# One step a turn, one edge buffer: a graph layer's kernel on one core

## The reference, cut to what matters

```
agg = segment_sum(edge_attr_48, dst, 12500)          # 412500 edges x 48, dst is sorted
h   = relu(layernorm(x))                             # x: 12500 nodes x 128
in_ = concat([h, agg, graph_globals[0]], axis=1)     # 128 + 48 + 64 columns
out = x + relu(in_ @ W1 + b1) @ W2 + b2              # hidden 256, out 128, all fp32
```

## Time and profile before

| | us |
|---|---|
| median of 3 runs | 277.42 |
| the profiled execution | 277.42 |
| its span | 275.7 |
| busy: TensorE, VectorE, ScalarE, GpSimd | 243.9, 241.4, 146.3, 75.4 |

### The profile page before, as it was taken

One profiled execution on the slowest core, in us unless ns is written; L12 is line 12 of the kernel. 1 busy time (PEld: TensorE's weight loads), 2 busy tenths in 40 slices (PEclk: granted clock), 3 DMA queues, 4 the chain that ended last, 5 costly groups with the idle time before them and its releaser, 6 DMA issues.

```text
span 275.7 us, 17264 instructions
## 1 busy us (share of the span) xinstructions
PE 243.9 (88%) x7448; PEld 195.3 (71%) x7448; DVE 241.4 (88%) x579; ACT 146.3 (53%) x315; POOL 75.4 (27%) x89
## 2 busy tenths in 40 slices
PE   7344869989999999799999999999999998999893
PEld 5234757687787788588778778877887796787572
DVE  2977699979879998999999999999999999886394
ACT  3712156566577564556455555655565555456640
POOL 8473010402113203203302312311330330334210
PEclk9955599999999999999999999999999999999999
DMA  7999999999999999999999999999999999982101
GB/s 247 370 381 379 336 382 385 360 330 382 390 387 387 392 389 386 378 390 387 390 394 386 386 393 388 384 389 386 367 391 390 386 372 375 387 291 88 40 38 57
DMA packets 70876, 94.53 MB, mean 343 GB/s; under 512 B 4324, under 2 KB 64260, under 8 KB 70854
## 3 DMA queue, kind: packets, MB, share of 16 engines
q1 hardware_dynamic: 69802, 94.29, 95.6%
q10 hardware_dynamic: 956, 0.00, 0.2%
q0 software_dynamic: 96, 0.00, 0.0%
HBM read 87.88 MB, written 6.40 MB: 342 GB/s over the span
## 4 chain that ended last, share of the span: by engine, by line
DMA 60%; PE 16%; DVE 12%; issue 5%; SPq 2%; POOL 1%; ACT 0%; DVEq 0%; POOLq 0%
DMA out<-out_buf 56%; PE group_bank L1020 6%; DVE onehot L777 5%; DMA x_buf<-in_x 3%; PE out_bank L1086 3%; SPq L327 2%; PE hidden_bank L1068 2%; PE window_bank L1043 2%; DVE rel_rows L732 2%; POOL out_buf L514 1%; DMA dst_rows<-in_dst 1%; DVE tile_sums L840 1%; DVE bn L819 1%; PE hidden_bank L1004 1%; DVE placing L789 1%
## 5 line engine op out<-in xcount | busy, mean ns | idle before, releaser
L777 DVE TENSOR_TENSOR onehot<-rel,const_bank 128x896 f32<-128x896 f32 (+1 forms) x122 | 122.8, 1026 | 8.1 <-PE group_bank L1020 8.0
L1020 PE MATMUL group_bank<-edge_buf,onehot 128*32 128x48 f32 x6454 | 87.1, 211 | 9.9 <-DVE onehot L777 5.8
L1020 PEld LDWEIGHTS group_bank<-edge_buf,onehot 128*32 128x32 f32 x6454 | 79.9, 113 | 22.2 <-issue 12.3
L514 POOL TENSOR_TENSOR out_buf<-mlp_out,xb_buf 128x512 f32<-128x512 f32 x23 | 29.6, 1288 | 166.0 <-DMA out<-out_buf 137.1
L1068 PE MATMUL hidden_bank<-normed_t,w_node 128*128 128x512 f32 (+1 forms) x100 | 51.6, 597 | 0.8 <-issue 0.7
L1086 PE MATMUL out_bank<-w_sb,hidden 128*128 128x128 f32 x384 | 47.7, 277 | 1.4 <-ACT normed_t L587 1.4
L1086 PEld LDWEIGHTS out_bank<-w_sb,hidden 128*128 128x128 f32 x384 | 44.7, 192 | 1.6 <-issue 1.6
L576 ACT ACTIVATE normed_x<-x_buf,shift,inverse 128x128 f32<-128x128 f32 x98 | 40.3, 482 | 9.7 <-DVE shift L834 9.7
L1072 PE MATMUL hidden_bank<-tile_sums,w_high 112*128 112x512 f32 (+1 forms) x50 | 39.0, 781 | 0.0
L502 POOL TENSOR_TENSOR xb_buf<-x_buf,b_rows 128x512 f32<-128x512 f32 (+1 forms) x25 | 31.6, 1267 | 19.8 <-DMA x_buf<-in_x 10.3
L608 ACT ACTIVATE hidden<-hidden_bank,hidden_bias 128x512 f32<-128x512 f32 (+1 forms) x50 | 32.3, 670 | 4.3 <-PE hidden_bank L1074 4.2
(11 more groups left out here) (92 smaller groups left out, 218.1 us busy)
## 6 DMA issues: line engine op xcount, KB each, us to landing
edge_buf<-in_edge_attr SPq DMA_DIRECT2D x97, 672.0 KB, 10.4
edge_buf<-in_edge_attr SPq DMA_DIRECT2D x24, 504.0 KB, 10.3
x_buf<-in_x SPq DMA_DIRECT2D x24, 256.0 KB, 8.9
out<-out_buf SPq DMA_DIRECT2D x23, 256.0 KB, 9.4
dst_rows<-in_dst SPq DMA_DIRECT2D x3, 448.5 KB, 7.8
dst_rows<-in_dst SPq DMA_DIRECT2D x1, 252.3 KB
out<-out_buf SPq DMA_DIRECT2D x1, 224.0 KB
edge_buf<-in_edge_attr SPq DMA_DIRECT2D x1, 168.0 KB, 9.2
```

The lines of the kernel that those rows point to most:

```text
L514: pool.tensor_tensor(out_buf[k.parity][:, 0:nj, :], mlp_out[:, 0:nj, :], xb_buf[k.third][:, 0:nj, :], ALU.add).then_inc(out_added, 1)
L777: dve.tensor_tensor(onehot[:, c0:c0 + cols, :], rel[:, r0:r0 + cols].unsqueeze(2).to_broadcast([P, cols, WINDOW]), ramp_const.unsqueeze(1) ...
L1020: done = pe.matmul(group_bank[h][WINDOW * j:WINDOW * (j + 1), n * F_EDGE:(n + 1) * F_EDGE], onehot[:, (g0 + j) * EDGES_PER_ROW + r, :], ed ...
```

## The change: what it does

- There is one edge buffer. `load_quad(s, q)` waits for the use of quad q in step s-1.
- TensorE's loop has 24 turns of one step. Conditions on the turn's number pick what the first two turns do otherwise. The first layer of tile s-2 now comes before `turn_x` of tile s-1.
- `hidden`, `normed_t` and `tile_sums` are single, but for a copy of tile 23's; ScalarE waits for the layers of the tile before, and copies the turned x after `relu_hidden`.
- There are 16 output buffers, with a semaphore each; `add_out` waits for the store 16 tiles back.
- At step s SP issues part 0 of step s+1, the x tile s+1, the store of tile s-4, part 1 of step s+1. The index blocks 1 to 3, b2 and the weights are loaded among the quads of step 1 and the x tile of tile 1.
- The index blocks 1 to 3 are made relative, turned and copied in steps 0 and 1; TensorE turns them at the end of these.
- `tile_low` runs on GpSimd in steps 2 to 23, ahead of `add_out`; the last three stay on VectorE.
- VectorE loads the two window positions of a step ahead of its fifth one-hot, and its opening order changes.
- The opening matmuls on ones (`keep_clock`) become a loop.

```diff
...
-        self.value = c + 2 * i if self.static else i * 2 + c
+        self.value = i + c
...
-        edge_buf = [sb(f"edge_buf{p}", [P, GROUPS, ROW]) for p in range(2)]
+        edge_buf = sb("edge_buf", [P, GROUPS, ROW])
...
-        out_buf = [sb(f"out_buf{p}", [P, NJ, F_NODE]) for p in range(2)]
+        out_buf = [sb(f"out_buf{n}", [P, NJ, F_NODE]) for n in range(OUT_SLOTS)]
...
+        def own(k):
+            return 1 if k.static and k.value == tiles - 2 else 0
...
-                if not s.below(2):
-                    sp.wait_ge(edges_used, s.plus(-2).value * NQ + q + 1)
+                if not s.below(1):
+                    sp.wait_ge(edges_used, s.plus(-1).value * NQ + q + 1)
...
-            load_part(At(1), 0)
-            load_part(At(1), 1)
             sp.dma_start(b2_rows[:, :], bass.AP(tensor=b2.tensor, offset=0, ap=[[0, P], [1, F_NODE]]))\
               .then_inc(b2_in, 16)
+            load_dst(1)
+            load_part(At(1), 0)
+            load_weights()
+            load_part(At(1), 1)
+            load_dst(2)
             load_x(At(1))
-            for s in range(steps):
-                if s >= 1 and s + 1 < tiles:
+            load_dst(3)
+            for s in range(1, steps):
+                if s + 1 < steps:
+                    load_part(At(s + 1), 0)
+                if s < tiles - 1:
                     load_x(last_tile() if s + 1 == tiles - 1 else At(s + 1))
-                if s + 2 < steps:
-                    load_part(At(s + 2), 0)
-                if s == 0:
-                    load_weights()
-                if s >= 4:
+                if 4 <= s < full_steps:
                     store(At(s - 4))
-                if s + 2 < steps:
-                    load_part(At(s + 2), 1)
-                if 1 <= s + 1 < blocks:
-                    load_dst(s + 1)
+                if s + 1 < steps:
+                    load_part(At(s + 1), 1)
...
-                elif not k.below(2):
-                    pool.wait_ge(stored[k.parity], k.turn * 16)
+                elif not k.below(OUT_SLOTS):
+                    pool.wait_ge(stored[slot(k)], k.value // OUT_SLOTS * 16)
...
             for s in range(steps):
+                if 2 <= s < full_steps:
+                    pool.wait_ge(xb_ready, s)
+                    tile_low(At(s - 2))
+                    pool.wait_ge(tile_low_ready, s + 1)
                 if s >= 3:
                     add_out(At(s - 3))
...
             copy_sums(At(0), 1)
+            relative(1)
             deviate(At(0))
             normalise(At(0))
+            copy_rel(1)
             copy_sums(At(1), 0)
             copy_turned(At(0))
+            bias()
             deviate(At(1))
+            relative(2)
             copy_sums(At(1), 1)
             normalise(At(1))
+            copy_rel(2)
+            relative(3)
+            copy_rel(3)
             for s in range(2, full_steps):
...
-                copy_turned(At(s - 1))
-                if s == 2:
-                    bias()
                 deviate(At(s))
                 relu_hidden(At(s - 2))
+                copy_turned(At(s - 1))
                 copy_sums(At(s), 1)
...
-                if s >= 2:
-                    tile_low(At(s - 2))
                 moments(At(s))
...
                 make_onehot(n, 3)
+                base = [window_base(At(s), h) for h in range(2)]
                 make_onehot(n, 4)
...
-                for _ in range(n):
+                with pe.Fori(0, n):
                     pe.matmul(bank[:, 0:2 * P], ones16[:, 0:P], ones16[:, :], start=True, stop=True)
...
-            with pe.Fori(0, full_steps // 2) as i:
...
+            with pe.Fori(0, full_steps) as i:
+                step = At(0, i)
+                sum_part(step, 0)
+                with pe.If(i > 1):
+                    place(step.plus(-1), 1)
+                    pe.wait_ge(rel_ready, 2 * blocks)
+                    first_layer(step.plus(-2))
+                    turn_x(step.plus(-1))
+                with pe.Else():
+                    with pe.If(i > 0):
+                        place(At(0), 1)
+                        turn_x(At(0))
+                        sum_bias()
+                    with pe.Else():
+                        turn_places()
+                sum_part(step, 1)
+                place(step, 0)
+                with pe.If(i > 1):
+                    second_layer(step.plus(-2))
+                with pe.Else():
+                    pe.wait_ge(bias_ready, i * 2 + 1)
+                    turn_rel(i + 1)
+                    with pe.If(i > 0):
+                        turn_rel(3)
...
```

More of the change, by code:

```diff
@@ L19 @@
 LAST_GROUPS = 5
+OUT_SLOTS = 16
 TILE = 512
@@ L183, in gnn_kernel @@
         b2_in = sem("b2_in")
[L184 removed]
+        edges_in = [sem(f"edges_in{q}") for q in range(NQ)]
         x_in = [sem(f"x_in{p}") for p in range(2)]
[L186 removed]
+        stored = [sem(f"stored{n}") for n in range(OUT_SLOTS)]
         last_stored = sem("last_stored")
@@ L276, in agg_tile, with before_own, slot, stores_of @@
             return agg[:, :, bass.ds(tile_strip(k), P)]
+        def own(k):
+            return 1 if k.static and k.value == tiles - 2 else 0
+        def before_own(k):
+            return k.value - 1 if k.value_is_last and k.static else k.value
+        def slot(k):
+            return k.value % OUT_SLOTS if k.static else 0
+        def stores_of(n):
+            return len(range(n, tiles - 1, OUT_SLOTS)) + (n == (tiles - 2) % OUT_SLOTS)
         def sums_tile(k, row):
-            sums = tile_sums[k.parity][row:row + F_EDGE, 0:strips_of(k) * P]
+            sums = tile_sums[own(k)][row:row + F_EDGE, 0:strips_of(k) * P]
             if k.value_is_last:
@@ L399, in _ @@
             store_last(last_tile(), last_stored)
-            sp.wait_ge(stored[0], 16 * (tiles // 2))
-            sp.wait_ge(stored[1], 16 * (tiles // 2) + 16)
+            for n in range(OUT_SLOTS):
+                sp.wait_ge(stored[n], stores_of(n) * 16)
             sp.wait_ge(last_stored, 16)
@@ L550, in copy_rel @@
                                    .rearrange("p (r g) -> p r g", g=P)[:, :, 0:rows], ACT.Copy)\
-                        .then_inc(rel_ready, 2 * steps if (b, h) == (blocks - 1, 1) else 1)
+                        .then_inc(rel_ready, 1)
             def copy_sums(s, h):
@@ L595, in tile_high @@
                     act.wait_ge(agg_added, min(2 * k.value + 3, all_adds) + 3)
-                    if not k.below(2):
-                        act.wait_ge(hidden_ready, 2 * k.value - 2)
+                    if not own(k):
+                        act.wait_ge(hidden_ready, 2 * before_own(k))
                 act.activation(sums_tile(k, 0), agg_tile(k), ACT.Copy).then_inc(tile_high_ready, 1)
@@ L602, in relu_hidden @@
                     act.wait_ge(out_ready, k.value)
-                elif not k.below(2):
-                    act.wait_ge(out_ready, k.value - 1)
+                elif not own(k):
+                    act.wait_ge(out_ready, before_own(k))
                 for c in range(2):
@@ L915, in _ @@
             make_placing(At(steps - 1), 0)
+            last_base = window_base(At(steps - 1), 0)
+            dve.wait_ge(tile_low_ready, tiles - 3 + 2)
             tile_low(At(tiles - 3))
@@ L918, in _ @@
             invert(last)
-            add_window(At(full_steps - 1), 1)
+            add_window(At(full_steps - 1), 1, base[1])
             low_sums(At(steps - 1), 0)
-            add_window(At(steps - 1), 0)
+            add_window(At(steps - 1), 0, last_base)
             tile_low(second)
@@ L938, in _ @@
                 dve.sem_inc(general_added, 1)
-                dve.wait_ge(stored[0], 16 * (tiles // 2))
-                dve.wait_ge(stored[1], 16 * (tiles // 2) + 16)
+                for n in range(OUT_SLOTS):
+                    dve.wait_ge(stored[n], stores_of(n) * 16)
                 dve.wait_ge(last_stored, 16)
@@ L1035, in place @@
                 pe.wait_ge(placing_ready[h], s.value + 1)
-                if not s.below(1) or h == 1:
+                if not s.below(1):
                     pe.wait_ge(agg_added, s.value * 2 + h + 2)
```

139 lines of the change are left out of this document (58 added, 81 removed).

## The result

The changed kernel takes 284.25 us (median of 4 runs, 283.99 to 284.85) where the kernel before takes 277.51 beside it: ratio 1.0244, interval 1.0221 to 1.0266. It is slower, by 6.7 us; forecast were 270.8, and at most 279.5.

What follows compares the result with a forecast made beforehand. The prediction took the one load/store queue and TensorE to limit in turns, with TensorE trailing the loads by a step at the end. 277.42 - 6.6, all other parts at 0, gave 270.8 us; range 266 to 279.5.

Steps and rivals of the forecast that it cites:

- I cost the single buffer at nothing in the steady state.: Edge loads after the opening: one buffer costs 0, since a backlog keeps the queue from running dry.
- The slower rival: Edge queue: fewer loads under way carry 370 GB/s, giving 279.8 us; slower from 374 GB/s down; chance 0.17.
- So step 2 starts at 37, as before.: Opening: x tile 1 lands at about 27 us, the chain after it ends at 37.1; bounds 34 to 41.
- 79.1 MB, at 386 GB/s.: Queue from 37.7 us to step 23's last quad: takes 204.9 us, to 242.6; landing 244.3, loop end 247.3.
- the balance of the prediction: Within one step: quads come free at 0.7 to 7.1 us, so the queue is never dry, by 0.4 to 0.9.
- TensorE trails the edge loads by a full step at the end: Loop end: TensorE would stand right behind the loads instead, ending at 247.3 rather than 253.86, -6.6 us.
- Low sums on GpSimd 0, sixteen output buffers 0.: VectorE and GpSimd: moving the low sums gains 0 (above, 21 us lost); dropping GpSimd's store waits gains 0.
- One step a turn 0.: TensorE's loop: 24 jumps back instead of 12 cost 0; above stands 4.49 us for each of 12 more turns.
- The closing 21.8 us.: After the loop's end: the closing work of 21.8 us stays as it was.
- compute: Rival: the queue beats 386 GB/s and TensorE's 9.42 us step rules, loop end 244.2, 267.8 us; chance 0.16.
- the x tile: Rival: it lands late and stalls VectorE, 0.3 us a step in 21 steps, 277 us; chance 0.14, half still faster.
- the jumps: Rival: TensorE's added loop jumps stall as in the first pass, 12 x 4.49 = 54 us, 325 us; chance 0.03.

Runs made afterwards that it cites:

- e13: The kernel before with three output buffers and the low sums of tiles 0 to 21 on GpSimd instead of VectorE: 278.06 us.
- e7: The changed kernel with two edge buffers, loads two steps ahead, two steps a turn and three output buffers: 279.69 us.
- e8: The changed kernel with two edge buffers, two steps a turn, three output buffers and three opening edits (matmuls written out, index blocks 2 and 3 later, x tile 1 first): 278.23 us.
- e14: The kernel before with one edge buffer, loads one step ahead, and the low sums of tiles 0 to 21 on GpSimd: 281.75 us.
- e9: The kernel before with a third output buffer, nothing else: 285.98 us.
- e4: The changed kernel with opening matmuls written out, index blocks 2 and 3 prepared in steps 2 and 3, and x tile 1 loaded ahead of the weights: 283.49 us.

## Why the prediction was wrong

Three runs lead from one kernel to the other: before 277.5; low sums on GpSimd and three output buffers 278.1 (e13, +0.6); the rest of the change but for the edge buffer 279.7 (e7, +1.6); the single edge buffer, with one step a turn and sixteen output buffers in place of three, 284.25 (+4.6). The +1.6 goes with the opening's order as far as e8 shows, which takes 1.5 of it back (278.2).

- **"I cost the single buffer at nothing in the steady state."** Nearly right: 382 GB/s from 60 to 240 us, quads landing after 7.9 us, TensorE waiting 5.3 us in all for edges from 60 to 258 us. The lower rate costs 1.7 us here. The slower rival (a rate under 374) did not happen here; e14 came to it from 60 to 150 us, with 370, and carried 388 afterwards.
- **"So step 2 starts at 37, as before."** This step failed, at 41.15. The x tile came at 30.4, not 27. The prediction's own terms give 27.9 (20.7 + 5.5 + 1.7), so 0.9 was a slip; for the rest, the queue carried 312 GB/s from 20.7 to 30.4 us in place of the 380 assumed. From the tile to the shift VectorE took the 4.43 us forecast, and then the chain ran as laid out, but for turning block 3, which took 1.77 us at the half clock and not 0.86. So 3.4 of the 4.1 us are the tile's and 0.7 the rest of the chain's; the 3.15 us that TensorE stood idle in its first turn do not lie on it. My bound was 41, but I gave a start there no price: with one buffer, a late step 2 is an empty queue.
- **"79.1 MB, at 386 GB/s."** Failed with it. The first quad of step 3 was issued at 42.56, not 37.7 (4.9 us). From 42.5 to 60 us the queue carried 298 GB/s, 1.5 MB or 4.0 us less than at 386, with the second dry spell in it: the balance of the prediction has the fourth quad free 6.5 us into a step, here it was issued at 8.9 (50.09). From 60 us to the last edge landing 381 GB/s in place of 386 are 2.5 us. From 42.5 us to that landing 80.4 MB were moved, not 79.1; half of the difference stands in the prediction as the landing's 1.7 us, the other half is 1.7 us more. With 0.3 at the loop's end these make up the 13.4 us by which the loop ends later than forecast. And the earlier trace rows should have warned me: 358 until 62 us, where I put 386 from 37.7.
- **"TensorE trails the edge loads by a full step at the end", -6.6 us.** Before, the last edge load of step 23 (the second of the two below) was issued at 236.80 and landed 10.0 us later, at 246.8; the loop ended at 253.9, 7.1 behind it. Of the 6.6 us, 4.1 were to come from standing nearer to that landing (3.0 instead of 7.1), and 3.8 came: it ends 3.3 behind. The other 2.5 rested on a last landing at 244.3, and it came at 257.4. SP's timeline of before:

```profile
235.80 2.82 SPq L327 DMA_DIRECT2D edge_buf<-in_edge_attr  x2
```

- **Low sums on GpSimd 0, sixteen output buffers 0.** Together +0.6 (e13, with three buffers), so the sum was nearly right by luck, by two errors that cancel: a third buffer alone is worth +8.5, the low sums with it -7.9. My account looked for who waits for GpSimd and missed that its wait for the store kept two engines apart. The hint was in the earlier trace rows: 685 ns is the median of L840, but 1540 its longest.
- **One step a turn 0.** Right in the steady state: from 60 to 240 us TensorE stood idle 6.2 us before its edge matmuls, 4.2 of it for loads and 1.9 for VectorE, none for an issue. Only the first pass shows gaps.
- **The closing 21.8 us.** Right.

The rivals: compute never came last; the x tile cost 6.2 us of VectorE's time from 60 to 240 us without setting the end; the jumps did not stall. The slow case came true through the opening, which I had as a bound and not as a rival; a step 2 after 41 was one of the signs of being wrong that I had named.

What stays open: writing out the clock-keeping matmuls (e1) made the opening later by way of x tile 1, which SP issued at 23.50 us instead of 21.84 and which landed 1.44 us later, as much as step 2 started later; why SP came to it later is not shown. Nor is it shown why the queue carried only 312 GB/s while that tile was under way in the kernel after, or why a single buffer carries 1 to 2% less once the opening is over.

## What to carry to other kernels

Before a buffer is given up, price the opening: with the queue as the limit, each MB that is not moved ahead costs its full transfer time (3 MB here, 7.9 us), and the steady state shows little of it (1 to 2% of the rate). A wait that seems to cost nothing may hold two engines apart; when one is removed, look for the instruction pairs that will now meet, and read the longest duration of a line, not its median. When a part costs nothing by two large effects, test each alone.

## What the hardware showed unexpectedly

VectorE and GpSimd shut each other out for whole instructions, in some operations. In the kernel before, a 0.16 us instruction of VectorE met GpSimd's add; VectorE's and GpSimd's timelines:

```profile
95.93 1.27 DVE L834 SCALAR_TENSOR_TENSOR shift<-mean_var,inverse 128x4 f32<-128x4 f32 x1
...
95.91 1.27 POOL L502 TENSOR_TENSOR xb_buf<-x_buf,b_rows 128x512 f32<-128x512 f32 x1
```

Both end at 97.2. Of the 25 such instructions of that kernel 12 start inside a GpSimd add and end 0.01 to 0.07 us after it, the others take 0.16. A low sum needs 0.685 us and ends 0.55 after the add, this one needs 0.16 and ends 0.02 after it: by both, an estimate, VectorE goes on 0.14 us before the add's recorded end. One-hot building, with one input in `const_bank`, a PSUM bank, was not touched: 1032 ns a piece before, 1034 in e9. The Trainium skill (SBUF — State Buffer, SBUF: two separate sides) says that the port pair which the two share is an exclusive lock, held for the whole instruction, and that a VectorE operation with two SBUF inputs wants it against a GpSimd operation that reads SBUF. The trace agrees in each of these cases: some 1.35 us for a low sum that starts inside an add, 0.685 outside one, and no change for the one-hot.

Fourteen single matmuls in a hardware loop at the start took 5.51 us, written out 3.17. And an engine that is let go earlier can come out later: in e4 step 2 began 7 us earlier, met loads that had not landed, and TensorE's granted clock was 0.50 from 35 to 44 us, the lower of its two levels (1.2 GHz of 2.4), with a first layer of twice the length.
